# Four PSUM banks for attention's scores and two for the maxima, in place of three and three

## Reference

```python
o1 = _attn(q, k1, v1, causal)          # branch 0: all earlier tokens
o2 = _attn(q, ks, vs)                  # branch 1: 256 selected tokens
o3 = _attn(q, kw, vw, winmask)         # branch 2: the last 64 tokens
o = g[:, 0] * o1 + g[:, 1] * o2 + g[:, 2] * o3
return o.reshape(B, T, N_HEAD * VDIM) @ Wproj
```

## Time and profile before

| | us |
|---|---|
| median of 3 executions | 2943.45 (2938.68 to 2945.27) |
| the profiled execution | 2938.53 |
| its span in the trace | 2936.4 |
| attention, from the first block's scores to the end of the last | about 795 to 2554 |
| the block that the rows below are from | 1237 to 1679.4 |

### The profile page before, as it was taken

How to read it: one execution, slowest core, us unless ns; L and a number is a source line. 1 busy time by engine, 2 the same in 40 slices (tenths; PEclk the granted TensorE clock), 3 DMA queues, 4 the chain that set the end, 5 groups by cost and what they waited for, 6 DMA issues and landing times. The chain is left out here.

```text
span 2936.4 us, 47406 instructions
## 1 busy us (share of the span) xinstructions
PE 2361.4 (80%) x16660; PEld 1563.1 (53%) x16660; DVE 1690.2 (58%) x3159; ACT 1219.0 (42%) x2665; POOL 536.5 (18%) x575
## 2 busy tenths in 40 slices
PE   5666766665499999799999799999899999630896
PEld 3444535443365666465666465666465665320785
DVE  4754847466455664555665555665555665450676
ACT  2323423233054554354554355455355455410442
POOL 0230504215000110100110100110100110136332
PEclk9777877877699999899999899999899999855997
DMA  2361715427846556446556446556546643241113
GB/s 91 139 243 36 288 58 211 170 89 293 183 102 131 122 125 128 106 102 136 122 119 126 106 104 137 127 109 126 115 104 131 132 104 73 91 84 48 48 51 109
DMA packets 222999, 361.11 MB, mean 123 GB/s; under 512 B 68810, under 2 KB 124717, under 8 KB 222384
## 3 DMA queue, kind: packets, MB, share of 16 engines
q1 hardware_dynamic: 218448, 349.72, 47.7%
q0 software_dynamic: 4320, 8.43, 0.9%
HBM read 230.10 MB, written 126.56 MB: 121 GB/s over the span
## 5 line engine op out<-in xcount | busy, mean ns | idle before, releaser
L1342 ACT ACTIVATE prob<-ps 128x512 f32<-128x512 f32 (+5 forms) x1600 | 637.5, 441 | 740.8 <-PE ps L1293 587.5
L1395 DVE TENSOR_REDUCE maxima<-ps 128x1 f32<-128x512 f32 (+3 forms) x768 | 387.1, 547 | 299.2 <-PE ps L1224 151.2
L1314 PE MATMUL ps<-prob,plain 128*32 128x512 f32 (+5 forms) x3200 | 512.1, 443 | 0.0
L1400 DVE TENSOR_REDUCE maxima<-ps 128x2 f32<-128x512 f32 (+1 forms) x512 | 294.5, 607 | 245.0 <-PE ps L1232 98.6
L1365 POOL TENSOR_TENSOR products<-products,sums 128x256 f32<-128x256 f32 x192 | 140.7, 733 | 1611.3 <-DVE sums L1386 1610.1
L1386 DVE RECIPROCAL sums<-sums 128x256 f32<-128x256 f32 x192 | 331.5, 1736 | 104.2 <-ACT sums L1353 104.2
L1285 PE MATMUL ps<-q1a_s,k1a_s 128*128 128x512 f32 (+3 forms) x768 | 303.1, 395 | 0.0
L1293 PE MATMUL ps<-q1b_s,k1b_s 128*128 128x512 f32 (+3 forms) x768 | 301.1, 393 | 0.0
L1314 PE MATMUL ps<-prob,v_s 128*32 128x512 f32 (+3 forms) x1536 | 284.3, 491 | 0.0
L1221 PE MATMUL ps<-k1a_s,q1a_s 128*128 128x512 f32 (+3 forms) x768 | 233.3, 372 | 8.7 <-DMA k1a_s<-k1ah_dram 8.3
L1285 PEld LDWEIGHTS ps<-q1a_s,k1a_s 128*128 128x128 f32 x768 | 147.1, 192 | 126.8 <-issue 118.1
(11 more groups left out here) (329 smaller groups left out, 4774.3 us busy)
## 6 DMA issues: line engine op xcount, KB each, us to landing
qh_dram<-pairs SPq DMA_DIRECT2D x96, 512.0 KB, 3.7
kwh_dram<-pairs SPq DMA_DIRECT2D x64, 512.0 KB, 2.7
qa_s<-qh_dram SPq DMA_DIRECT2D x128, 256.0 KB, 4.5
kwa_s<-kwh_dram SPq DMA_DIRECT2D x128, 256.0 KB, 7.6
q1a_s<-qh_dram SPq DMA_DIRECT2D x128, 256.0 KB, 4.7
qb_s<-qh_dram SPq DMA_DIRECT2D x64, 256.0 KB, 9.2
kwb_s<-kwh_dram SPq DMA_DIRECT2D x64, 256.0 KB, 10.0
k1a_s<-k1ah_dram SPq DMA_DIRECT2D x32, 512.0 KB, 6.8
```

Source lines behind the costliest of these rows:

```text
L1314: mm = pe.matmul(ps[at:at + VD, SCORES + k % 2, q0 - c * CH:q0 - c * CH + w], w_, m.prob[:, n % PROBS, h, 0:w], start=first, stop=True, sk ...
L1342: act.activation(m.prob[:, u % PROBS, h, 0:w], ps[:, turn % SCORES, 0:w], ACT.Exp, scale=SCALE).then_inc(s["exp_done"], 1)
L1395: ins = dve.tensor_reduce(partial[:, h, i, part:part + 1], bank[:, 0:w], AX, ALU.max)
L1400: ins = dve.tensor_reduce(negs[1 if kind == "max1" else 2][:, at:at + 2], bank.rearrange("p (i n) -> p i n", i=2)[:, :, 0:w], AX, ALU.max, ...
```

## The change

The constants of the split are exchanged. Nothing is added, removed or moved in the list of steps. The two banks of the running sums become 4 and 5 (before 3 and 4).

```diff
-SCORES = 3
-SPARES = 3
+SCORES = 4
+SPARES = 2
```

## The result

The median of four executions is 3092.89 us (3089.78 to 3096.11), against 2942.52 us for the kernel before on the same chip. The ratio is 1.0512, with an interval of 1.0493 to 1.0531: 5.1% slower, as forecast in size and sign. The profiled execution took 3096.11 us, its span is 3094.0 us.

A forecast was written before the change was run, and what follows sets the result against it. PE was taken to bound attention. Odd passes cost 7.9 us, even 2.8, a block's first 0.9; three full blocks 122.7, CLOSING 30, OPENING 1, together 154 over 2938.5: 3092, with half of 5 added 3095 us (8-in-10 range 3045 to 3145).

The forecast's parts named there:

- max1 fill behind the rows copy: Odd pass, near 1306.17: the fill's bank waits for the turned rows' copy behind a reciprocal; PE stands 2.0 us.
- max0 fill, before 1313.82: Odd pass, fill at 1313.82: needs the first of two reductions from 1314.71, done at 1315.33; 1.6 us lost.
- max0 fill, before 1328.92: Odd pass, fill at 1328.92: needs the first, short one of three reactions by DVE (reductions) from 1329.80; 1.2 us lost.
- max0 fill, before 1330.87: Odd pass, second matmul from 1330.51: waits for a reduction done near 1333.02; 2.2 us, 0.8 already paid, so 1.4.
- small stops and DVE's slip: Odd pass: four smaller fill stops of 0.4 to 0.6 us, 1.8 in all, plus 0.5 as DVE slips further at 1303.7.
- unloaded weights: A stopped fill finds its weights unloaded: 0.1 us per new stop, 0.5 us in an odd pass, 0.4 in an even one.
- score turns: The fourth score bank removes PE's waits for exponentials, the whole gained: 1.1 us in an odd pass, 0.8 in an even one.
- Rival 1: Clock falls too: 4 to 9 us at 1.2 GHz in each of 15 odd passes, DVE keeps up; 3130 us, chance 0.17.
- Rival 2: Smaller stops are absorbed because DVE has caught up after each stop, so next fills find free banks; 3020 us, chance 0.14.
- Rivals 3 and 4: Third: fills not stopped, the gain stays alone, 2905 us, chance 0.03. Fourth: nothing changes, chance 0.03.
- OPENING: The part in which PE and DVE only pass fills to each other: 1 us more.
- CLOSING: Part with three odd passes with fills: 33.0 us less about 3 for its last pass, so 30 us more.

The follow-up runs named there:

- the kernel with three and two: Against the changed kernel, spare banks stay at two but score banks are three instead of four, one bank unused; 3104.83 us, ratio 1.0550 to the kernel before.
- four and two with short pieces: The changed kernel (four score, two spare banks) with each inversion in four pieces of 128 columns instead of two of 256; 2980.64 us, ratio 1.0125.

## Why the prediction was right, step by step

The total, 154 us over the profiled execution, came out as 157.6. Below that, the large stops were read nearly exactly: that is the mechanism, and it was right. That the total came within 4 us is partly luck, because smaller terms were mis-sized and cancelled. Without a fall of the clock an odd pass cost 7.2 us (forecast 7.9) and an even one 1.9 (2.8), some 21 us less than forecast over 15 and 12 passes. The falls of the clock, which the sum put at nothing, cost some 28 us more. For the odd pass, the steps of the two passes aligned by their starts (before from 1396.4, after from 1454.4, us):

| term of the sum | forecast | measured |
|---|---|---|
| max1 fill behind the rows copy | 2.0 | 1.98 |
| max0 fill, before 1313.82 | 1.6 | 1.32 |
| max0 fill, before 1328.92 | 1.2 | 1.15 |
| max0 fill, before 1330.87 | 1.4 | 1.42 |
| small stops and DVE's slip | 2.3 | 2.56 |
| unloaded weights | 0.5 | 0.30 |
| score turns | -1.1 | -1.35 |
| proj | 0 | -0.33 |
| clock | 0 | +1.5 |
| other small differences | 0 | about +0.1 |
| sum | 7.9 | 8.6 |

- The rule by which a fill was called late (the end of DVE's reading of fill n-2, plus 0.05 us) held: the largest stop ended 0.06 us after the copy. It told the places of stops as well. All four small ones came: those near 1294.4, 1303.7, 1316.7 (the fill of the rows, L1250) and 1324.0, with 0.44, 0.89, 0.32 and 0.40 us. The forecast had no fifth. It is a max1 fill (before at 1418.59, after at 1479.30), late by 0.51 us only because of the sooner score turn ahead of it.
- The gain was read right at the turns (1.1 forecast, 1.35 measured), but its place in the sum was wrong. "The whole is gained" holds for waits on ACT alone. In the odd pass the next stopped fill took it back, as the kernel with three and two showed. The forecast took DVE's moments from the trace before, so a turn that came sooner made no fill late in its sum.
- Proj was overlooked: it stood already, for POOL's multiplication with the inverses. In the even pass PE's start of proj at 1351.92 had 0.91 us of idle time before it in the trace of before, and POOL's last multiplication, which proj waits for in the code, ended 0.11 us ahead of it, at 1351.81. The profile puts this wait down to DVE. After, the 1.18 us stop ahead of it used 0.69 of this up. So the even pass cost 1.9 us, not 2.8. Its stops summed to 3.24 us (forecast 3.2), its turns to -0.88 (-0.8).
- Rival 1, the clock, happened in part, and in addition to the forecast. Inside the blocks, 11 of the 12 odd passes that aren't at a border had one or two falls, 14 in all. At 1.5 us each (61.6 us with one, 60.1 with none, 63.2 with two) that is 21 us, and the border passes grew by 9 to 11 us where 7.2 is a pass without a fall, another 7. These 28 us are an estimate from the lengths of the passes. By the forecast's own list of signs ("if the granted clock inside a pass fell below 1.00") this is where it was wrong. Rival 1 said 4 to 9 us at the lower clock; it was some 3.4 us (0.57 over the 4 us shown). Its guess that DVE would then keep up was wrong: the waits of the pass with a fall and of that without are the same to 0.1 us.
- Rival 2, absorbed small stops, did not happen. The four that were foreseen came with 2.05 of 2.3 us. Rivals 3 and 4 are excluded by the 33.7 us in a block in which PE's matmuls waited for DVE (the forecast said some 50).
- The forecast's view that the reciprocals make the odd pass dear is shown by the pair without them (108 of 151 us) and by the pieces of 128 columns (90 of 151 us), where DVE's busy time stays and only the length of its instructions and their places change. Both numbers hold the falls of the clock too.
- The smaller terms: OPENING cost 1.7 us (1 forecast), the three full blocks 43.5, 42.5 and 41.2 (40.9), CLOSING 28 (30).

The remark of the Trainium skill weighed in the forecast, TensorE: Matmul & The Clock Gate, section "A second HAM failure mode: psum-queue depth-cycling", agrees with after: with short idle times of PE at PSUM banks in the passes the clock swung between its two levels, which cost some 28 us of 151. In the trace with short pieces, where PE also stops at those banks but for 1.0 us at most, it did not.

## What to carry to other kernels

Here a pool of PSUM banks had to be as deep as its reader's queue was long at the worst place, and that length was set by instructions that have nothing to do with the bank. So split the long instruction (two of 256 columns into four of 128 gave back 112 us) before taking a bank for it, and read the depth fill by fill from "may n start when n-2 is emptied", which here gave each of the four large stops to 0.3 us. It missed one stop of 0.5 us, because it took the moments from the trace before. A wait removed ahead of a stop that stays is not a gain; count it only up to the next point at which the engine waits for something else. When banks are scarce, look for the pool whose users can be set apart by order alone (the sums, here), not for the one with the smallest waits today.

## What the runs showed of the hardware

The clock fell inside passes in which PE stands for at most 1.8 us at a time. Over 1478 to 1482, PE was busy for 2.50 us of 4.00 at full clock; over 1482 to 1486 it was busy throughout at a granted clock of 0.57, its first scores matmul taking 0.80 us (0.49 for the same one before, at 1314.88). Away from the blocks' borders, the changed kernel's trace has 18 falls in odd passes, each of 3.4 us. They began 0.2 to 1.2 us after the end of a stop: seven after the one of 1.8 us, eleven after the one of 1.15 us at the first max0 fill. But the same stops don't always do it. The pass from 2539.5 has the same waits as that from 1454.4 (1.8, 1.2 and 0.6 us before L1232 and L1221, 2.5 us in three at L1395) and no fall. In the block of the kernel with three and two that is shown above, two of the three odd passes that don't touch a border had none. With stops of 1.0 us at most (four and two with short pieces), no pass inside a block had one. What decides between the passes alike in their waits stays open; no run was made for it.

A reciprocal of 128x256 took 1.74 us and one of 128x128 0.94 us, one of 128x64 0.52 us: pieces of 128 columns cost DVE only 25 us more than those of 256 in before, over attention, for 192 more instructions, and the odd pass's busy time rose by 0.1 us.
